# The row maximum of a causal attention taken over the newest 512 keys of a chunk, on a signal of its own

## The chip, the cores and the metric

The kernel runs on one core of a Trainium2 chip. The metric is the device time in microseconds (us) of one execution, the median of several.

## The reference

One transformer block with adaptive layer norm on 4096 rows of 256 channels. The attention has 16 heads of 16 channels. What matters here:

```python
h = layernorm(x) * (1 + ca) + sa
q, k, v = split(h @ W_attn)                      # 16 heads of 16 channels, T = 4096
att = softmax(where(causal, q @ k.T / 4, -inf))
att = att * decay_weight_matrix(T)               # 0 from a distance of 512 on
y = (att @ v) @ W_proj
x = x + ga * y                                   # then a second layer norm and a linear layer
```

The softmax sums over all earlier keys, but the decay matrix is 0 beyond a distance of 511, so values are needed for the newest 5 blocks of 128 keys alone.

## The kernel before

Queries are handled in 32 tiles of 128 rows. `attention_fast` works on pairs of tiles: pair p joins a FAR tile (16 + p, which sees 17 + p blocks of 128 keys) with a NEAR tile (15 - p, which sees 16 - p blocks). For each pair and each of 16 heads there is one step, 16 x 16 = 256 steps in all, numbered s. In a step the keys of both tiles are cut into five chunks of at most 1024 keys (`split`, `order`): the newest chunk of the FAR tile first (FAR, 0), an older one of it (FAR, 1), the newest of the NEAR tile (NEAR, 0), and two more older ones. The newest chunk has at least 5 blocks where there are that many: 640 columns for the FAR tile of pairs 0 to 4 and 8 to 12, 768 for pairs 5 and 13, 896 for 6 and 14, 1024 for 7 and 15.

All engines run a list written out by hand, in step order:

- TensorE (PE), `fill` (L839): one chunk of scores into one of three slots of PSUM (`s_ps`, `SLOTS` = 3, each 1024 fp32 columns, two banks of 512), in matmuls of at most 512 columns. Chunk n waits (`exp_done`) until ScalarE is done with chunk n - 3. The newest chunk ends with a 128-column matmul (L856) that adds the causal mask to its last block. Then `s_full` is raised. Between the fills stand the transposes of the exponentials (`turn` L871 for three blocks, `turn_tail` L887 for the other two), in every second step the products with the values for a group of four heads (`values`, L902, in two parts), and the jobs that finish the pair before (projection, second norm, linear layer; L913, L923, L931, L944).
- VectorE (DVE), `maximum` (L1076): waits for `s_full`, then a minimum over the last 640 columns of the newest chunk (the scores carry a negative scale), L1082, and raises `max_done`. `decay` (L1091) and `decay_tail` (L1101) multiply the transposed exponentials by the decay while they move them out of PSUM. The order in a step is: maximum FAR of step s; decay and decay_tail of NEAR of step s - 1; maximum NEAR of s; small jobs; decay FAR of s; a copy of a finished group (L1107) or another job; decay_tail FAR of s.
- ScalarE (ACT), `exponential` (L1011, L1029): one activation for each chunk, with the maximum as bias and a sum over the row. That of a newest chunk waits for `max_done` and for the transposes of the step before, and writes `probs` in SBUF; the others wait for `s_full` and write back into the slot.

The maximum only keeps the exponentials within the range of fp32. The sums over a row are compared with SUM_LIMIT = 1e37 at the end; if one is above, `attention_full` and `rest_full` compute everything again (`again > 0`).

```python
dve.wait_ge(s_full, n + 1)
nc.vector.tensor_reduce(out=negmax[:, p % 2, side, h:h + 1],
                        in_=s_ps[:, n % SLOTS, max(0, cols - P * WIN):cols],
                        axis=AX_X, op=ALU.min).then_inc(max_done, 1)
```

Of the kernel before, what the change touches and what calls it, by code (L numbers as in the profile page):

```python
# [5 lines left out]
def bass_adaln_block_kernel(nc, x, w_attn, w_proj, ffn_wT, ffn_b, lora_downT, lora_upT, down_aux, up_auxT,  # L6
# [18 lines left out]
    P = 128  # L25
# [3 lines left out]
    NH, HD = 16, 16  # L29
# [12 lines left out]
    BANK = 512  # L42
    CW = 2 * BANK
    RING = 3
    WIN = 5
# [149 lines left out]
    with ctx:  # L195
# [3 lines left out]
        def sem(name):  # L199
            return ctx.enter_context(nc.semaphore(name))  # L200
# [426 lines left out]
        def attention_fast():  # L627
# [22 lines left out]
            def split(i):  # L650

                nb = i + 1
                n = -(-nb // CB)
                first = nb if n == 1 else max(WIN, nb - CB * (n - 1))
                cuts = [(nb - first, nb)]
                left = nb - first
                while left > 0:
                    cuts.append((max(0, left - CB), left))
                    left = cuts[-1][0]
                return cuts  # L660

            def order(p):

                if len(split(tile_of(p, NEAR))) == 1:
                    return [(FAR, 0), (FAR, 1), (NEAR, 0), (FAR, 2), (FAR, 3)]
                return [(FAR, 0), (FAR, 1), (NEAR, 0), (NEAR, 1), (FAR, 2)]
# [60 lines left out]
            vals_loaded = [sem(f"fast_vals_loaded{b}") for b in range(2)]  # L727
            decay_loaded = sem("fast_decay_loaded")
            s_full = sem("fast_s_full")
            max_done = sem("fast_max_done")  # L730
            exp_done = sem("fast_exp_done")
            turn_full = sem("fast_turn_full")
# [24 lines left out]
            with s2:  # L757
# [80 lines left out]
                def _(pe):  # L838
                    def fill(s, pos):  # L839

                        p, h = step_of(s)
                        side, c = order(p)[pos]
                        i = tile_of(p, side)
                        n = PER * s + pos
                        if n >= SLOTS:
                            pe.wait_ge(exp_done, n - SLOTS + 1)
                        b0, b1 = split(i)[c]
                        cols = P * (b1 - b0)
                        q = q_stack[:, s // QH % 2, side, s % QH, :]
                        for o in range(0, cols, BANK):  # L850
                            w = min(BANK, cols - o)
                            diag = c == 0 and o + w == cols
                            last = nc.tensor.matmul(s_ps[:, n % SLOTS, o:o + w], q, k_stack[:, h, P * b0 + o:P * b0 + o + w],  # L853
                                                    start=True, stop=not diag)
                            if diag:
                                last = nc.tensor.matmul(s_ps[:, n % SLOTS, o + w - P:o + w], ident_b[:], causal[:],  # L856
                                                        start=False, stop=True)
                        last.then_inc(s_full, 1)

                    def turn(side, s):  # L860
# [148 lines left out]
                @block.scalar  # L1009
                def _(act):  # L1010
                    def exponential(s, pos):  # L1011
                        p, h = step_of(s)
                        side, c = order(p)[pos]
                        n = PER * s + pos
                        b0, b1 = split(tile_of(p, side))[c]
                        cols = P * (b1 - b0)
                        src = dst = s_ps[:, n % SLOTS, 0:cols]
                        if c == 0:
                            act.wait_ge(max_done, 2 * s + side + 1)
                            if s > 0:  # L1020

                                if has_tail(side, s - 1):
                                    act.wait_ge(tail_full, tail_no["unit", side, s - 1] + 1)
                                else:
                                    act.wait_ge(turn_full, turn_no["unit", side, s - 1] + 1)
                            dst = probs[:, side, 0:cols]
                        else:
                            act.wait_ge(s_full, n + 1)
                        nc.scalar.activation(dst, src, ACT.Exp, bias=negmax[:, p % 2, side, h:h + 1], scale=-1.0,  # L1029
                                             accum_out=sums[:, p % 2, side, h, c:c + 1]).then_inc(exp_done, 1)  # L1030

                    for s in range(NSTEP):
                        for pos in range(PER):
                            exponential(s, pos)
# [35 lines left out]
                def _(dve):  # L1070
# [5 lines left out]
                    def maximum(side, s):  # L1076
                        p, h = step_of(s)
                        n = PER * s + order(p).index((side, 0))
                        dve.wait_ge(s_full, n + 1)
                        b0, b1 = split(tile_of(p, side))[0]  # L1080
                        cols = P * (b1 - b0)
                        nc.vector.tensor_reduce(out=negmax[:, p % 2, side, h:h + 1],  # L1082
                                                in_=s_ps[:, n % SLOTS, max(0, cols - P * WIN):cols],
                                                axis=AX_X, op=ALU.min).then_inc(max_done, 1)

                    def decay(side, s):
# [809 lines left out]
```

## Time and profile before

| what | value |
| --- | --- |
| median of 3 runs | 1506.9 us (1505.77 to 1508.43) |
| the profiled execution | 1504.86 us |
| its span, first to last instruction | 1502.3 us |
| ScalarE busy | 1298.8 us (86%) |
| TensorE matmuls busy | 1263.3 us (84%) |
| VectorE busy | 1000.9 us (67%) |
| first and last exponential start | 164.66 us, 1466.46 us |

The first 165 us are the layer norm, the projections and the splitting of q and k into bf16 parts; the last 35 us finish the last pair. Between them run the 256 steps of attention. A line number such as L1082 is a line of the kernel before. "PE" rows are matmuls, "PEld" rows are weight loads. A row of the timeline gives start, duration, engine, line and operation, and in brackets how long the engine had been idle before it and what ended that.

### The profile page before, as it was taken

Reading aid. Unit: us, or ns where it says so; the run is one execution under the profiler, and the core shown is the slowest. Engines: PE = TensorE matmul, PEld = TensorE weight load, DVE = VectorE, ACT = ScalarE, POOL = GpSimd, SP = SyncE. Lnnn points to the kernel's source line nnn. Section 1 sums busy time; section 2 is a strip of 40 time slices with the busy share of each in tenths; the row PEclk is TensorE's granted clock in tenths of the full one; section 3 lists DMA queues with packets and bytes.
Section 4 is the critical chain, followed back from the end, with each engine's and each line's share of the span. In section 5 each row is a group of like instructions: output and inputs, shape, how many; then the busy total and the mean of one; then the engine's idle time right before and its main releaser. Section 6 shows DMA issues by size and latency. Waiting matters only on the chain.

```text
span 1502.3 us, 28806 instructions
## 1 busy us (share of the span) xinstructions
PE 1263.3 (84%) x11067; PEld 745.0 (50%) x11067; DVE 1000.9 (67%) x2058; ACT 1298.8 (86%) x2628; POOL 204.2 (14%) x429
## 2 busy tenths in 40 slices
PE   7994588989888898888888998988898888887774
PEld 5552345555555555555555555555555444444432
DVE  4843477777777777777777777777776766665452
ACT  2552699999999999999999999999999999999880
POOL 0331000110202020202011020202020201111022
PEclk9996799999999999999999999999999999999996
DMA  4797300000000000000000000000000000000000
GB/s 154 240 302 263 106 12 12 19 26 19 15 19 14 23 19 26 19 25 19 26 19 23 17 14 22 16 26 19 26 16 25 15 26 15 26 15 19 8 4 13
DMA packets 94448, 64.63 MB, mean 43 GB/s; under 512 B 59595, under 2 KB 89570, under 8 KB 94306
## 3 DMA queue, kind: packets, MB, share of 16 engines
q1 hardware_dynamic: 94306, 62.75, 14.1%
q8 instruction: 87, 1.43, 0.4%
q14 instruction: 55, 0.45, 0.1%
HBM read 41.74 MB, written 20.97 MB: 42 GB/s over the span
## 4 chain that ended last, share of the span: by engine, by line
PE 39%; DVE 27%; ACT 13%; issue 9%; POOL 1%; SPq 0%; DMA 0%; ACTq 0%; DVEq 0%
PE fast_s_ps L853 13%; DVE fast_negmax L1082 12%; PE fast_t_ps L902 10%; ACT fast_s_ps L1029 8%; DVE fast_probsT L1101 7%; PE fast_t_ps L871 5%; PE fast_t_ps L887 5%; ACT fast_probs L1029 5%; PE fast_t_ps L931 4%; DVE fast_probsT L1091 4%; DVE fast_y_sb L1120 1%; DVE fast_xb L1134 1%; DVE fast_xb L1157 1%; PE fast_t_ps L913 1%; DVE fast_tT L1127 1%
## 5 line engine op out<-in xcount | busy, mean ns | idle before, releaser
L1029 ACT ACTIVATE fast_s_ps<-fast_s_ps,fast_negmax 128x1024 f32<-128x1024 f32 (+4 forms) x768 | 786.6, 1026 | 12.4 <-PE fast_s_ps L853 11.7
L853 PE MATMUL fast_s_ps<-k_stack,fast_q_stack 96*128 96x512 bf16 (+3 forms) x2448 | 643.2, 354 | 118.1 <-ACT fast_probs L1029 83.5
L1029 ACT ACTIVATE fast_probs<-fast_s_ps,fast_negmax 128x640 f32<-128x640 f32 (+7 forms) x512 | 431.7, 843 | 62.1 <-DVE fast_negmax L1082 57.8
L1082 DVE TENSOR_REDUCE fast_negmax<-fast_s_ps 128x1 f32<-128x640 f32 (+4 forms) x512 | 397.9, 777 | 35.9 <-PE fast_s_ps L856 20.2
L1091 DVE TENSOR_TENSOR fast_probsT<-fast_t_ps,fast_dec_c 128x384 f32<-128x384 f32 (+2 forms) x512 | 276.6, 540 | 202.8 <-PE fast_t_ps L871 202.7
L853 PEld LDWEIGHTS fast_s_ps<-k_stack,fast_q_stack 96*128 96x128 bf16 x2448 | 202.4, 98 | 321.4 <-ACT fast_probs L1029 137.2
L871 PE MATMUL fast_t_ps<-ident,fast_probs 128*128 128x128 f32 x1488 | 252.0, 276 | 29.4 <-DVE fast_y_sb L1120 20.8
L1101 DVE TENSOR_TENSOR fast_probsT<-fast_t_ps,fast_dec_c 128x256 f32<-128x256 f32 x464 | 192.4, 415 | 114.7 <-PE fast_t_ps L887 114.7
L871 PEld LDWEIGHTS fast_t_ps<-ident,fast_probs 128*128 128x128 f32 x1488 | 171.8, 142 | 84.1 <-DVE fast_y_sb L1120 28.1
L887 PE MATMUL fast_t_ps<-ident,fast_probs 128*128 128x128 f32 x912 | 195.9, 295 | 19.9 <-DVE fast_tT L1127 6.4
L902 PE MATMUL fast_t_ps<-fast_probsT,fast_vals 128*16 128x128 f32 x4800 | 179.8, 275 | 23.4 <-DVE fast_probsT L1101 21.9
L1029 ACT ACTIVATION_READ_ACCUMULATOR fast_s_ps<-fast_s_ps,fast_negmax 128x1 f32 x768 | 163.6, 213 | 0.0
L1048 POOL TENSOR_SCALAR fast_var_e<-fast_mv 128x1 f32<-128x1 f32 x32 | 7.3, 228 | 1129.5 <-DVE fast_mv L1142 1129.4
L887 PEld LDWEIGHTS fast_t_ps<-ident,fast_probs 128*128 128x128 f32 x912 | 97.2, 141 | 118.7 <-DVE fast_yT_sb L1107 47.9
L902 PEld LDWEIGHTS fast_t_ps<-fast_probsT,fast_vals 128*16 128x16 f32 x4800 | 109.1, 96 | 71.3 <-DVE fast_probsT L1101 45.8
L856 PE MATMUL fast_s_ps<-causal,ident_b 128*128 128x128 bf16 x512 | 113.3, 221 | 0.0
L1029 ACT ACTIVATION_READ_ACCUMULATOR fast_probs<-fast_s_ps,fast_negmax 128x1 f32 x512 | 104.2, 203 | 0.0
L856 PEld LDWEIGHTS fast_s_ps<-causal,ident_b 128*128 128x128 bf16 x512 | 49.8, 97 | 54.9 <-issue 1.4
L392 ACT CAST part<-kq 128x2048 bf16<-128x2048 f32 x8 | 15.2, 1898 | 39.7 <-issue 20.2
L404 POOL TENSOR_TENSOR part<-kq,part 128x2048 bf16<-128x2048 f32 (+1 forms) x8 | 32.0, 4000 | 103.2 <-ACT part L392 103.2
L1054 POOL TENSOR_SCALAR fast_rstd<-fast_root_t,fast_three_halves,fast_rstd 128x1 f32<-128x1 f32 x128 | 44.0, 344 | 12.9
L1053 POOL TENSOR_SCALAR fast_root_t<-fast_rstd,fast_var_h 128x1 f32<-128x1 f32 x128 | 44.0, 344 | 12.9
(110 smaller groups left out, 723.7 us busy)
## 6 DMA issues: line engine op xcount, KB each, us to landing
parts_d<-part SPq DMA_DIRECT2D x24, 512.0 KB, 4.3
k_stack<-parts_d SPq DMA_DIRECT2D x96, 128.0 KB, 3.0
fast_q_stack<-parts_d SPq DMA_DIRECT2D x384, 32.0 KB, 2.1
fast_vals<-v_d SPq DMA_DIRECT2D x36, 128.0 KB, 2.5
xs<-x_dram SPq DMA_DIRECT2D x8, 512.0 KB, 6.6
v_d<-w SPq DMA_DIRECT2D x8, 512.0 KB, 5.7
fast_xb<-x_dram SPq DMA_DIRECT2D x32, 128.0 KB, 2.1
out_dram<-fast_xb SPq DMA_DIRECT2D x32, 128.0 KB, 2.0
```

The lines of the kernel that those rows point to most:

```text
L853: last = nc.tensor.matmul(s_ps[:, n % SLOTS, o:o + w], q, k_stack[:, h, P * b0 + o:P * b0 + o + w], start=True, stop=not diag)
L856: last = nc.tensor.matmul(s_ps[:, n % SLOTS, o + w - P:o + w], ident_b[:], causal[:], start=False, stop=True)
L871: last = nc.tensor.transpose(t_ps[:, P * b:P * (b + 1)], probs[:, side, lo:lo + P], ident[:])
L887: last = nc.tensor.transpose(tail_ps[:, P * (b - HEAD):P * (b - HEAD + 1)], probs[:, side, lo:lo + P], ident[:])
L902: last = nc.tensor.matmul(g_ps[TC * j:TC * j + HD, :], vals[:, side, (i + 1 - nb + b) % VT, HD * (h + j):HD * (h + j + 1)], probsT[:, turn ...
L931: last = nc.tensor.matmul(tail_ps[:, 0:C], tT[:, side, cc, :], weights[:, cc, :], start=(cc == 0), stop=(cc == CH - 1))
L1029: nc.scalar.activation(dst, src, ACT.Exp, bias=negmax[:, p % 2, side, h:h + 1], scale=-1.0, accum_out=sums[:, p % 2, side, h, c:c + 1]).th ...
L1053: chained(nc.gpsimd.tensor_scalar(w, y, y, half, ALU.mult, ALU.mult))
L1054: chained(nc.gpsimd.tensor_scalar(y, w, three_halves[:, 0:1], y, ALU.add, ALU.mult))
L1082: nc.vector.tensor_reduce(out=negmax[:, p % 2, side, h:h + 1], in_=s_ps[:, n % SLOTS, max(0, cols - P * WIN):cols], axis=AX_X, op=ALU.min) ...
L1091: nc.vector.tensor_tensor(probsT[:, turned(side, s), 0:n, :], t_ps[:, 0:P * n].rearrange("p (b q) -> p b q", q=P), dec_c[:, WIN - nb:WIN - ...
L1101: nc.vector.tensor_tensor(probsT[:, turned(side, s), HEAD:nb, :], tail_ps[:, 0:P * (nb - HEAD)].rearrange("p (b q) -> p b q", q=P), dec_c[ ...
```

## The change

In a newest chunk the columns now lie at the end of the slot (CW - cols to CW) and no longer at its start. The matmul over its newest 512 columns comes first, then the causal mask; if the chunk has more than 4 blocks, a new semaphore `new_full` is raised there, and a matmul over the older columns follows, after which `s_full` is raised. The maximum waits for `new_full` instead of `s_full` and reads the newest 512 columns instead of 640. The exponential of such a chunk waits for `s_full` too. Tiles whose newest chunk has at most 4 blocks keep their wait. Older chunks are filled as before.

```diff
--- before.py
+++ after.py
@@ -659,6 +659,19 @@
                     left = cuts[-1][0]
                 return cuts
 
+            MAXW = BANK // P
+
+            def has_older_part(s, side):
+
+                b0, b1 = split(tile_of(s // NH, side))[0]
+                return b1 - b0 > MAXW
+
+            new_no = {}
+            for s in range(NSTEP):
+                for side in (FAR, NEAR):
+                    if has_older_part(s, side):
+                        new_no[side, s] = len(new_no)
+
             def order(p):
 
                 if len(split(tile_of(p, NEAR))) == 1:
@@ -727,6 +740,7 @@
             vals_loaded = [sem(f"fast_vals_loaded{b}") for b in range(2)]
             decay_loaded = sem("fast_decay_loaded")
             s_full = sem("fast_s_full")
+            new_full = sem("fast_new_full")
             max_done = sem("fast_max_done")
             exp_done = sem("fast_exp_done")
             turn_full = sem("fast_turn_full")
@@ -847,14 +861,21 @@
                         b0, b1 = split(i)[c]
                         cols = P * (b1 - b0)
                         q = q_stack[:, s // QH % 2, side, s % QH, :]
-                        for o in range(0, cols, BANK):
-                            w = min(BANK, cols - o)
-                            diag = c == 0 and o + w == cols
-                            last = nc.tensor.matmul(s_ps[:, n % SLOTS, o:o + w], q, k_stack[:, h, P * b0 + o:P * b0 + o + w],
-                                                    start=True, stop=not diag)
-                            if diag:
-                                last = nc.tensor.matmul(s_ps[:, n % SLOTS, o + w - P:o + w], ident_b[:], causal[:],
-                                                        start=False, stop=True)
+
+                        def scores(at, k0, w, stop=True):
+                            return nc.tensor.matmul(s_ps[:, n % SLOTS, at:at + w], q, k_stack[:, h, k0:k0 + w], start=True, stop=stop)
+
+                        if c > 0:
+                            for o in range(0, cols, BANK):
+                                last = scores(o, P * b0 + o, min(BANK, cols - o))
+                            last.then_inc(s_full, 1)
+                            return
+                        w = min(BANK, cols)
+                        scores(CW - w, P * b1 - w, w, stop=False)
+                        last = nc.tensor.matmul(s_ps[:, n % SLOTS, CW - P:CW], ident_b[:], causal[:], start=False, stop=True)
+                        if has_older_part(s, side):
+                            last.then_inc(new_full, 1)
+                            last = scores(CW - cols, P * b0, cols - BANK)
                         last.then_inc(s_full, 1)
 
                     def turn(side, s):
@@ -1014,9 +1035,11 @@
                         n = PER * s + pos
                         b0, b1 = split(tile_of(p, side))[c]
                         cols = P * (b1 - b0)
-                        src = dst = s_ps[:, n % SLOTS, 0:cols]
+                        src = dst = s_ps[:, n % SLOTS, CW - cols:CW] if c == 0 else s_ps[:, n % SLOTS, 0:cols]
                         if c == 0:
                             act.wait_ge(max_done, 2 * s + side + 1)
+                            if has_older_part(s, side):
+                                act.wait_ge(s_full, n + 1)
                             if s > 0:
 
                                 if has_tail(side, s - 1):
@@ -1076,11 +1099,13 @@
                     def maximum(side, s):
                         p, h = step_of(s)
                         n = PER * s + order(p).index((side, 0))
-                        dve.wait_ge(s_full, n + 1)
+                        if has_older_part(s, side):
+                            dve.wait_ge(new_full, new_no[side, s] + 1)
+                        else:
+                            dve.wait_ge(s_full, n + 1)
                         b0, b1 = split(tile_of(p, side))[0]
-                        cols = P * (b1 - b0)
                         nc.vector.tensor_reduce(out=negmax[:, p % 2, side, h:h + 1],
-                                                in_=s_ps[:, n % SLOTS, max(0, cols - P * WIN):cols],
+                                                in_=s_ps[:, n % SLOTS, CW - P * min(MAXW, b1 - b0):CW],
                                                 axis=AX_X, op=ALU.min).then_inc(max_done, 1)
 
                     def decay(side, s):
```

How the instructions move, first on TensorE. This is the start of a step: the fill of (FAR, 0), the transposes of NEAR of the step before, and the first matmul of the next fill (names ending in k_stack, q_stack are the score matmuls; causal, ident_b is the mask). Before:

```order
L853 MATMUL fast_s_ps<-k_stack,fast_q_stack 128x512 [waits fast_exp_done]
L853 MATMUL fast_s_ps<-k_stack,fast_q_stack 128x128
L856 MATMUL fast_s_ps<-causal,ident_b 128x128
L871 MATMUL fast_t_ps<-ident,fast_probs 128x128 [waits fast_turn_free]
L871 MATMUL fast_t_ps<-ident,fast_probs 128x128 x2
L887 MATMUL fast_t_ps<-ident,fast_probs 128x128 [waits fast_tail_free]
L887 MATMUL fast_t_ps<-ident,fast_probs 128x128
L853 MATMUL fast_s_ps<-k_stack,fast_q_stack 128x512 [waits fast_exp_done]
```

After:

```order
L866 MATMUL fast_s_ps<-k_stack,fast_q_stack 128x512 [waits fast_exp_done]
L875 MATMUL fast_s_ps<-causal,ident_b 128x128
L866 MATMUL fast_s_ps<-k_stack,fast_q_stack 128x128
L892 MATMUL fast_t_ps<-ident,fast_probs 128x128 [waits fast_turn_free]
L892 MATMUL fast_t_ps<-ident,fast_probs 128x128 x2
L908 MATMUL fast_t_ps<-ident,fast_probs 128x128 [waits fast_tail_free]
L908 MATMUL fast_t_ps<-ident,fast_probs 128x128
L866 MATMUL fast_s_ps<-k_stack,fast_q_stack 128x512 [waits fast_exp_done]
```

The mask has moved ahead of the 128 older columns; the number and the sizes of the matmuls, and all that follows, stay as they were.

On VectorE, the end of one step and the start of the next, where the maximum stands behind the group's copy and `decay_tail` FAR. Before:

```order
L1107 COPY fast_yT_sb<-fast_t_ps 128x128 [waits fast_tail_full]
L1101 TENSOR_TENSOR fast_probsT<-fast_t_ps,fast_dec_c 128x256 [waits fast_tail_full]
L1082 TENSOR_REDUCE fast_negmax<-fast_s_ps 128x1 [waits fast_s_full]
L1091 TENSOR_TENSOR fast_probsT<-fast_t_ps,fast_dec_c 128x384 [waits fast_turn_full]
L1101 TENSOR_TENSOR fast_probsT<-fast_t_ps,fast_dec_c 128x256 [waits fast_tail_full]
L1082 TENSOR_REDUCE fast_negmax<-fast_s_ps 128x1 [waits fast_s_full]
```

After:

```order
L1132 COPY fast_yT_sb<-fast_t_ps 128x128 [waits fast_tail_full]
L1126 TENSOR_TENSOR fast_probsT<-fast_t_ps,fast_dec_c 128x256 [waits fast_tail_full]
L1107 TENSOR_REDUCE fast_negmax<-fast_s_ps 128x1 [waits fast_new_full]
L1116 TENSOR_TENSOR fast_probsT<-fast_t_ps,fast_dec_c 128x384 [waits fast_turn_full]
L1126 TENSOR_TENSOR fast_probsT<-fast_t_ps,fast_dec_c 128x256 [waits fast_tail_full]
L1107 TENSOR_REDUCE fast_negmax<-fast_s_ps 128x1 [waits fast_new_full]
```

The place of the maximum in the list is the same; its wait is now for the first 512 columns.

On ScalarE, five exponentials in a row, two of them of newest chunks (they write fast_probs). Before:

```order
L1029 ACTIVATE fast_s_ps,fast_sums<-fast_s_ps,fast_negmax 128x1024 [waits fast_s_full]
L1029 ACTIVATE fast_probs,fast_sums<-fast_s_ps,fast_negmax 128x640 [waits fast_tail_full,fast_max_done]
L1029 ACTIVATE fast_s_ps,fast_sums<-fast_s_ps,fast_negmax 128x768 [waits fast_s_full]
L1029 ACTIVATE fast_s_ps,fast_sums<-fast_s_ps,fast_negmax 128x1024 [waits fast_s_full]
L1029 ACTIVATE fast_probs,fast_sums<-fast_s_ps,fast_negmax 128x768 [waits fast_tail_full,fast_max_done]
```

After:

```order
L1052 ACTIVATE fast_s_ps,fast_sums<-fast_s_ps,fast_negmax 128x1024 [waits fast_s_full]
L1052 ACTIVATE fast_probs,fast_sums<-fast_s_ps,fast_negmax 128x640 [waits fast_tail_full,fast_s_full,fast_max_done]
L1052 ACTIVATE fast_s_ps,fast_sums<-fast_s_ps,fast_negmax 128x768 [waits fast_s_full]
L1052 ACTIVATE fast_s_ps,fast_sums<-fast_s_ps,fast_negmax 128x1024 [waits fast_s_full]
L1052 ACTIVATE fast_probs,fast_sums<-fast_s_ps,fast_negmax 128x768 [waits fast_tail_full,fast_s_full,fast_max_done]
```

The two exponentials of newest chunks have one wait more.

## Rows read from the trace of the kernel before

**Rows 1.** The page, part 4: the chain that ended last, by line.

```profile
PE fast_s_ps L853 13%; DVE fast_negmax L1082 12%; PE fast_t_ps L902 10%; ACT fast_s_ps L1029 8%; DVE fast_probsT L1101 7%; PE fast_t_ps L871 5%; PE fast_t_ps L887 5%; ACT fast_probs L1029 5%; PE fast_t_ps L931 4%; DVE fast_probsT L1091 4%; DVE fast_y_sb L1120 1%; DVE fast_xb L1134 1%; DVE fast_xb L1157 1%; PE fast_t_ps L913 1%; DVE fast_tT L1127 1%
```

**Rows 2.** 243 to 1141 us: length, busy (x count) of PE, PEld, DVE, ACT, POOL, clock.

```profile
243.00:1141.20 898.20, 794.81 (x7713) 481.06 (x7712) 661.92 (x1332) 852.76 (x1761) 118.16 (x286) 1.00 0.08 20
```

**Rows 3.** Waits, whole span: who waited for whom, us in total, times, longest.

```profile
ACT fast_probs L1029 <- DVE fast_negmax L1082: 57.8, 141, 10.6
...
DVE fast_negmax L1082 <- PE fast_s_ps L856: 20.2, 52, 1.4
```

**Rows 4.** Timeline of ScalarE, 521 to 525 us (pair 4).

```profile
521.22 1.10 ACT L1029 ACTIVATE fast_s_ps<-fast_s_ps,fast_negmax 128x1024 f32<-128x1024 f32 x1
522.22 0.22 ACT L1029 ACTIVATION_READ_ACCUMULATOR fast_s_ps<-fast_s_ps,fast_negmax 128x1 f32 x1
522.72 0.80 ACT L1029 ACTIVATE fast_probs<-fast_s_ps,fast_negmax 128x640 f32<-128x640 f32 x1 [0.28 <-DVE fast_negmax L1082]
...
523.50 1.08 ACT L1029 ACTIVATE fast_s_ps<-fast_s_ps,fast_negmax 128x1024 f32<-128x1024 f32 x1
...
524.59 0.79 ACT L1029 ACTIVATE fast_probs<-fast_s_ps,fast_negmax 128x640 f32<-128x640 f32 x1
```

**Rows 5.** Timeline of ScalarE: (FAR, 0) and the row before, first and last of 255 steps.

```profile
168.71 0.67 ACT L1029 ACTIVATE fast_s_ps<-fast_s_ps,fast_negmax 128x512 f32<-128x512 f32 x1
...
169.66 0.79 ACT L1029 ACTIVATE fast_probs<-fast_s_ps,fast_negmax 128x640 f32<-128x640 f32 x1 [0.16 <-DVE fast_negmax L1082]
...
1461.59 1.10 ACT L1029 ACTIVATE fast_s_ps<-fast_s_ps,fast_negmax 128x1024 f32<-128x1024 f32 x1
...
1462.84 1.11 ACT L1029 ACTIVATE fast_probs<-fast_s_ps,fast_negmax 128x1024 f32<-128x1024 f32 x1
```

**Rows 6.** Chain in order of time, 516 to 529 us (pair 4): start, us, what.

```profile
516.83 0.73 DVE fast_negmax L1082
517.56 0.46 DVE fast_probsT L1091
518.03 0.34 DVE fast_probsT L1101
...
518.41 0.85 PE fast_t_ps L902 x24
...
521.52 0.42 DVE fast_probsT L1101
521.95 0.74 DVE fast_negmax L1082
...
522.72 0.22 ACT fast_probs L1029
...
523.66 0.55 PE fast_s_ps L853 x2
...
526.82 0.73 DVE fast_negmax L1082
...
528.40 0.85 PE fast_t_ps L902 x24
```

**Rows 7.** Lines by form, DVE: count, busy, mean ns, idle before.

```profile
L1082 DVE TENSOR_REDUCE fast_negmax<-fast_s_ps 128x1 f32<-128x640 f32 x448 | 366.7, 819 | 30.4 <-PE fast_s_ps L856 16.1 <-PE fast_s_ps L853 10.6
...
L1082 DVE TENSOR_REDUCE fast_negmax<-fast_s_ps 128x1 f32<-128x512 f32 x16 | 11.0, 686 | 0.2 <-PE fast_s_ps L856 0.2
```

**Rows 8.** Timeline of DVE, pair 4: decay_tail FAR, then the maximum FAR.

```profile
521.52 0.42 DVE L1101 TENSOR_TENSOR fast_probsT<-fast_t_ps,fast_dec_c 128x256 f32<-128x256 f32 x1 [0.53 <-PE fast_t_ps L887]
521.87 0.82 DVE L1082 TENSOR_REDUCE fast_negmax<-fast_s_ps 128x1 f32<-128x640 f32 x1
```

**Rows 9.** Timeline of PE, pair 4: the mask ahead of that maximum.

```profile
521.60 0.22 PE L856 MATMUL fast_s_ps<-causal,ident_b 128*128 128x128 bf16 x1
```

**Rows 10.** Timeline of DVE, pair 7 (1024 columns): decay_tail FAR, then the maximum.

```profile
787.89 0.42 DVE L1101 TENSOR_TENSOR fast_probsT<-fast_t_ps,fast_dec_c 128x256 f32<-128x256 f32 x1 [0.53 <-PE fast_t_ps L887]
788.38 0.82 DVE L1082 TENSOR_REDUCE fast_negmax<-fast_s_ps 128x1 f32<-128x640 f32 x1
```

## The prediction

> **What bounds the kernel now.** I read the chain of the page first, by line: the maximum (L1082) has 12% of it, though VectorE is busy for 67% of the span only [rows 1]. So a reduction on a half idle engine is part of what sets the time. Then the stretch of pairs 1 to 11: in 898.2 us ScalarE is busy for 852.8, 95%, TensorE's matmuls for 794.8, VectorE for 661.9, at a granted clock of 1.00, the 2.4 GHz level [rows 2]. ScalarE is nearly the bound, and what the change can give at most is what ScalarE still waits. The list of waits says for whom: exponentials of newest chunks for the maximum, 57.8 us, of which 10.6 is one wait at the very start; 47.2 us over 140 waits remain [rows 3].
>
> The timeline shows that the loss is larger than "idle". The activation at 521.22 ends at 522.32 and the next one starts at 522.72, a hole of 0.40, of which 0.28 is booked as idle, since the read of the accumulator (0.22 from 522.22) stands in it. Without a wait the next activation starts as the last one ends: 522.72 + 0.80 = 523.52 against a start at 523.50 [rows 4]. I took this hole ahead of (FAR, 0) for steps 1 to 255, from start times like those of the first and the last [rows 5], 0.28 and 0.15; the sum over the 255 is 76 us. The holes before (NEAR, 0), read in the same way, sum to under 2 us. **76 us is the ceiling.**
>
> The chain in order of time then says what makes (FAR, 0) late. In one step it runs: maximum FAR (516.83), decay and decay_tail of NEAR (517.56, 518.03), values (518.41), then TensorE's list without a gap up to decay_tail FAR (521.52), and again maximum FAR (521.95). In the next it runs from that maximum to the exponential (522.72), the fill that needs its slot (523.66), a projection, decay_tail, and the maximum at 526.82, after which decay, decay_tail and values (528.40) follow again [rows 6]. The loop of two steps holds **two maxima of the FAR tile**, and no maximum of the NEAR tile. ScalarE is in it for one exponential out of ten. So what comes off a FAR maximum comes off the period, until the holes on ScalarE are used up.
>
> **The change, part by part.** *The shorter reduction.* 640 columns take 819 ns (448 of them), 512 columns 686 ns (16 of them) [rows 7], so each of the 448 loses 0.133 us, 60 us of VectorE in all. The 192 on the NEAR side lie beside exponentials that don't wait, and count as 0; if the cover went, they would be worth 192 x 0.133 = 26 us more at most. On the FAR side it is one for each step: 256 x 0.133 = **34.0 us**.
>
> *The early signal.* In pair 4 decay_tail FAR starts at 521.52 and takes 0.42, and the maximum starts at 521.87, that is 0.07 before the end of that row [rows 8]; the mask ends at 521.82 [rows 9]. VectorE and TensorE arrive together, and VectorE is as early as it can be: an earlier signal gives nothing there. That is so in the ten pairs with 640 FAR columns, 160 steps. With 1024 columns the maximum starts 0.07 after the end of decay_tail (788.38 against 787.89 + 0.42 = 788.31) [rows 10], 0.14 later than in pair 4; with 896 and 768 columns I read about 0.10 and 0.04. There are two pairs of each, 32 steps: 32 x (0.14 + 0.10 + 0.04) = **9.0 us**. The end below is 0. The end above is that the 128-column matmul counts also in the 160 steps. The trace doesn't show it alone; two score matmuls start and end within 0.5 us, and I put it at 0.05: 8 us more.
>
> *Where ScalarE has no hole left.* Taking steps two by two, since the loop is of two, the gain is the smaller of both holes and twice the step's saving. Done for all 255 this costs 2.6 us against the two terms, mostly in pairs 13 and 14, where every second hole is near 0: **-2.6 us**.
>
> *The third wait.* The exponential of a newest chunk waits for `s_full` too, which has long come when the reduction ends: the rest of the fill is 128 to 512 columns, the reduction 0.69 us. What stays is the look at one semaphore more. No row shows a third wait; one with two starts 0.01 after the end of the one before (523.50 + 1.08, 524.59), one with a single wait 0.02 before it (522.72 + 0.80, 523.50) [rows 4]. I take 0.02 on the 139 exponentials that wait, **-2.8 us**, between 0 and, if it hit all 448, -9 us.
>
> *The rest.* The matmuls are as many and as wide, each with its own weight load as before; the order mask, older part instead of older part, mask costs nothing, and no DMA moves. Behind the mask on TensorE's queue nothing is later, since the whole fill takes as long. On VectorE the maximum has the same place; what is queued behind it (decay of NEAR, waited for by the values) comes 0.133 earlier, which is the gain itself.
>
> Sum: 34.0 + 9.0 - 2.6 - 2.8 = 37.6 us, 2.5%. The profiled execution took 1504.9 us (span 1502.3 and 2.6 around it): 1467.3. The median is 2.0 above it, so the forecast is **1469 us**. With the ends of the terms the gain lies between 34.0 - 2.6 - 9 = 22 and 34.0 + 9.0 + 8 = 51, 1456 to 1485. A difference under 0.2%, 3 us, could not be told from none.
>
> **A rule that speaks against it.** The rows name ScalarE as the busiest engine, and the change takes nothing off its work. The Trainium skill (Perfetto Trace Analysis, "Identifying the Most-Contended Engine") says to optimise the most-contended engine first, taken as the one with the highest occupancy. By that the sum would be 0 and the time 1506.9. The hole at 522.72, with the maximum named as what ends it [rows 4], is what speaks against the rule here.
>
> **The rivals.** *Only the visible waits shrink.* The period doesn't shrink with both maxima, since something else arrives just as late (the fill that waits for an exponential, or TensorE's list, 88% busy [rows 2]). Then each of the 140 waits [rows 3] loses 0.133 once: 19 us, 1488. For it: in most second steps the hole is 0.2 or less. Against: the chain has both maxima with nothing between them and the values.
>
> *Hidden.* ScalarE's neighbours fill the time again, 0 gained, 1507, as the rule on the busiest engine would have it.
>
> *All holes close.* The time gained moves TensorE's waits apart so that more than the maximum comes early: up to 76 us, 1431; a part of it, 60 us, is 1447. For it: none of the chain's pieces, only that waits of the kind "both arrive together" can give way in both directions.
>
> *Slower: the reduction is disturbed.* TensorE now writes the lower bank of the slot while VectorE reads the upper one. If that made the reduction of 512 columns take more than the 0.82 of now, the loop would be longer: at 0.92 by 256 x 0.10 = 26 us, 1533; the point is 0.82. Against: TensorE's matmuls are busy for 88% of the time [rows 2], so they write beside nearly all of today's reductions, which average 819 ns [rows 7] and take 0.82 in each row shown [rows 8, 10].
>
> *Slower: everything twice.* With a maximum over fewer keys a row's sum could pass 1e37, whose logarithm is 85.2, and the attention of at least 1300 us would run again, over 2800 us. I worked out the sums from the inputs and the reference's formulas: the largest logarithm is 61.9 with 5 blocks and 68.7 with 4. So it isn't taken.
>
> **How the numbers follow.** The loop as worked out: 0.67. Only the visible waits: 0.17. More than 51 us: 0.08. Hidden: 0.04. Disturbed: 0.03; twice: 0.01. Faster is 0.67 + 0.17 + 0.08 = 0.92, same 0.04, slower 0.04. The range takes the first case with its ends, 1456 to 1485, and the second, up to 1489; below I go to 1450, which takes in a small part of the third.
>
> **What would show it.** Reductions of 512 columns at 0.69 us. ScalarE's waits for the maximum down from 57.8 to about 30 us, the start of 10.6 included. The 16 steps of pair 4 shorter by about 2 us, those of pair 7 by over 4. The maximum in pair 7 starting 0.07 before the end of decay_tail, as in pair 4. No wait of the exponential for `s_full`. I am wrong if the chain no longer holds the maximum twice in two steps and the time is above 1489, if the reduction of 512 columns takes much over 0.69, or if the wide pairs gain no more than the narrow ones.

## The result and the profile after

The changed kernel takes 1463.0 us (median of 4 runs, 1459.68 to 1464.15), the kernel before on the same chip 1506.3. The ratio is 0.9715, with a 95% interval of 0.9696 to 0.9734: 43 us less, where 37.6 were forecast.

In what follows, "the changed kernel" is this one. Line numbers have moved with the change: the score matmuls are L866 (were L853), the mask L875 (L856), the transposes L892 and L908 (L871, L887), the values L923 (L902), the exponential L1052 (L1029), the maximum L1107 (L1082), decay and decay_tail L1116 and L1126 (L1091, L1101).

The chain by line, of the page of the kernel after, answers to [rows 1]:

```profile
PE fast_s_ps L866 14%; ACT fast_s_ps L1052 10%; ACT fast_probs L1052 9%; PE fast_t_ps L923 8%; DVE fast_negmax L1107 6%; PE fast_t_ps L892 6%; PE fast_t_ps L908 6%; DVE fast_probsT L1126 5%; PE fast_t_ps L952 4%; DVE fast_probsT L1116 3%; DVE fast_xb L1182 1%; DVE fast_y_sb L1145 1%; DVE fast_xb L1159 1%; DVE fast_tT L1152 1%; DVE fast_tT L1176 1%
```

The maximum has 6% of the chain, where it had 12%. The stretch of pairs 1 to 11, from the first exponential of pair 1 to that of pair 12, in the columns of [rows 2] (length, busy time and count of PE, PEld, DVE, ACT, POOL, clock, DMA share, GB/s):

```profile
242.96:1111.93 868.97, 794.78 (x7713) 483.06 (x7712) 612.41 (x1332) 847.29 (x1762) 117.44 (x286) 1.00 0.08 21
```

It is 869.0 us long instead of 898.2. TensorE and VectorE run as many instructions as before (7713 matmuls, 1332 rows), but VectorE is busy for 49.5 us less (612.4 against 661.9). ScalarE is busy for 97.5% of the stretch instead of 95. The waits that answer to [rows 3], and the reduction by form that answers to [rows 7]:

```profile
DVE fast_negmax L1107 <- PE fast_s_ps L875: 26.1, 63, 0.9
...
ACT fast_probs L1052 <- DVE fast_negmax L1107: 16.3, 57, 0.9
```

```profile
L1107 DVE TENSOR_REDUCE fast_negmax<-fast_s_ps 128x1 f32<-128x512 f32 x464 | 317.0, 683 | 25.3 <-PE fast_s_ps L875 13.4 <-DMA fast_dec_c<-decay_cols_dram 10.5
```

ScalarE waits 16.3 us for the maximum. Before, it was 47.2 without the one wait of 10.6 at the start, which the trace of the changed kernel books on another line. The reduction takes 683 ns instead of 819.

The chain in order of time again, at the same steps of pair 4 (as [rows 6]: start, us, what):

```profile
506.25 0.55 PE fast_s_ps L866 x2
...
507.17 0.56 DVE fast_probsT L1116
507.73 0.61 DVE fast_tT L1152
...
508.38 0.44 PE fast_t_ps L908 x2
...
509.19 0.96 ACT fast_s_ps L1052 x2
510.15 0.78 ACT fast_probs L1052 x2
510.93 1.09 ACT fast_s_ps L1052 x2
512.02 0.78 ACT fast_probs L1052 x2
512.80 1.38 ACT fast_s_ps L1052 x3
...
514.90 0.67 ACT fast_probs L1052
...
518.58 0.42 DVE fast_probsT L1126
519.00 0.60 DVE fast_negmax L1107
519.60 0.47 DVE fast_probsT L1116
520.07 0.34 DVE fast_probsT L1126
...
520.45 0.85 PE fast_t_ps L923 x24
```

Here the chain stays on ScalarE from 509.19 on, for one whole step of exponentials (0.45 us of it is booked as issue, in the rows left out). Before, in [rows 6], ScalarE was in it once in two steps. Where holes are left, the old loop is still seen: maximum (519.00), decay, decay_tail, values.

### The profile page after: what moved, and what is told of

It is laid out like the page before. It is cut to its first block, busy times and chain, and to the rows that moved or that the text cites. A ratio compares the mean times of both kernels' runs of the same rounds, so it can differ in the third digit from the quotient of the medians.

```text
span 1460.6 us, 28808 instructions
## 1 busy us (share of the span) xinstructions
PE 1260.3 (86%) x11067; PEld 747.5 (51%) x11067; DVE 936.9 (64%) x2058; ACT 1289.9 (88%) x2628; POOL 203.1 (14%) x429
## 4 chain that ended last, share of the span: by engine, by line
PE 39%; DVE 19%; ACT 19%; issue 5%; POOL 1%; ACTq 0%; DVEq 0%
PE fast_s_ps L866 14%; ACT fast_s_ps L1052 10%; ACT fast_probs L1052 9%; PE fast_t_ps L923 8%; DVE fast_negmax L1107 6%; PE fast_t_ps L892 6%; PE fast_t_ps L908 6%; DVE fast_probsT L1126 5%; PE fast_t_ps L952 4%; DVE fast_probsT L1116 3%; DVE fast_xb L1182 1%; DVE fast_y_sb L1145 1%; DVE fast_xb L1159 1%; DVE fast_tT L1152 1%; DVE fast_tT L1176 1%
## 5 line engine op out<-in xcount | busy, mean ns | idle before, releaser
L1052 ACT ACTIVATE fast_s_ps<-fast_s_ps,fast_negmax 128x1024 f32<-128x1024 f32 (+4 forms) x768 | 789.5, 1032 | 8.6 <-PE fast_s_ps L866 8.1
L866 PE MATMUL fast_s_ps<-k_stack,fast_q_stack 96*128 96x512 bf16 (+3 forms) x2448 | 667.9, 353 | 94.4 <-ACT fast_probs L1052 60.2
L1052 ACT ACTIVATE fast_probs<-fast_s_ps,fast_negmax 128x640 f32<-128x640 f32 (+7 forms) x512 | 433.8, 847 | 21.4 <-DVE fast_negmax L1107 16.3
L1116 DVE TENSOR_TENSOR fast_probsT<-fast_t_ps,fast_dec_c 128x384 f32<-128x384 f32 (+2 forms) x512 | 276.7, 540 | 221.2 <-PE fast_t_ps L892 221.1
L866 PEld LDWEIGHTS fast_s_ps<-k_stack,fast_q_stack 96*128 96x128 bf16 x2448 | 208.9, 98 | 337.2 <-ACT fast_probs L1052 112.8
L1107 DVE TENSOR_REDUCE fast_negmax<-fast_s_ps 128x1 f32<-128x512 f32 (+3 forms) x512 | 337.4, 659 | 38.3 <-PE fast_s_ps L875 26.1
L892 PE MATMUL fast_t_ps<-ident,fast_probs 128*128 128x128 f32 x1488 | 251.0, 275 | 28.0 <-DVE fast_y_sb L1145 19.4
L1126 DVE TENSOR_TENSOR fast_probsT<-fast_t_ps,fast_dec_c 128x256 f32<-128x256 f32 x464 | 192.5, 415 | 114.7 <-PE fast_t_ps L908 114.7
L892 PEld LDWEIGHTS fast_t_ps<-ident,fast_probs 128*128 128x128 f32 x1488 | 177.1, 141 | 78.0 <-DVE fast_y_sb L1145 26.5
L908 PE MATMUL fast_t_ps<-ident,fast_probs 128*128 128x128 f32 x912 | 195.5, 295 | 20.1 <-DVE fast_tT L1152 6.4
L923 PE MATMUL fast_t_ps<-fast_probsT,fast_vals 128*16 128x128 f32 x4800 | 179.7, 275 | 9.0 <-DVE fast_probsT L1126 4.5
L1052 ACT ACTIVATION_READ_ACCUMULATOR fast_s_ps<-fast_s_ps,fast_negmax 128x1 f32 x768 | 168.4, 219 | 0.0
L908 PEld LDWEIGHTS fast_t_ps<-ident,fast_probs 128*128 128x128 f32 x912 | 96.8, 141 | 118.5 <-DVE fast_yT_sb L1132 48.0
L923 PEld LDWEIGHTS fast_t_ps<-fast_probsT,fast_vals 128*16 128x16 f32 x4800 | 109.0, 96 | 56.3 <-DVE fast_probsT L1126 28.4
L875 PE MATMUL fast_s_ps<-causal,ident_b 128*128 128x128 bf16 x512 | 112.9, 220 | 0.0
L1052 ACT ACTIVATION_READ_ACCUMULATOR fast_probs<-fast_s_ps,fast_negmax 128x1 f32 x512 | 107.5, 210 | 0.0
L875 PEld LDWEIGHTS fast_s_ps<-causal,ident_b 128*128 128x128 bf16 x512 | 50.2, 98 | 16.0 <-issue 0.5
```

Source lines behind the costliest of these rows:

```text
L866: return nc.tensor.matmul(s_ps[:, n % SLOTS, at:at + w], q, k_stack[:, h, k0:k0 + w], start=True, stop=stop)
L875: last = nc.tensor.matmul(s_ps[:, n % SLOTS, CW - P:CW], ident_b[:], causal[:], start=False, stop=True)
L892: last = nc.tensor.transpose(t_ps[:, P * b:P * (b + 1)], probs[:, side, lo:lo + P], ident[:])
L908: last = nc.tensor.transpose(tail_ps[:, P * (b - HEAD):P * (b - HEAD + 1)], probs[:, side, lo:lo + P], ident[:])
L923: last = nc.tensor.matmul(g_ps[TC * j:TC * j + HD, :], vals[:, side, (i + 1 - nb + b) % VT, HD * (h + j):HD * (h + j + 1)], probsT[:, turn ...
L1116: nc.vector.tensor_tensor(probsT[:, turned(side, s), 0:n, :], t_ps[:, 0:P * n].rearrange("p (b q) -> p b q", q=P), dec_c[:, WIN - nb:WIN - ...
```

## The experiments

All of them are compared with the kernel before on the same chip; each ratio has its 95% interval. For the stretch of the 256 steps I also give how much shorter a pair of tiles is than before, from the start of its first exponential to the start of the next pair's (for pair 15, to the end of the last exponential). These lengths are read from the profiled execution of each kernel. A "narrow" pair has 640 columns in the newest FAR chunk, a "wide" one 768 to 1024.

### The shorter reduction without the signal of its own

```diff
-                        if has_older_part(s, side):
-                            dve.wait_ge(new_full, new_no[side, s] + 1)
-                        else:
-                            dve.wait_ge(s_full, n + 1)
+                        dve.wait_ge(s_full, n + 1)
```

> The changed kernel without its own signal: the maximum over 512 columns waits for the whole chunk again. Loop theory: nothing is lost in the ten pairs with 640 FAR columns, since decay_tail FAR on VectorE ends together with the fill; 32 x (0.14 + 0.10 + 0.04) = 9 us are lost in the six wide ones, so 1463 + 9 = 1472 us, and in pair 7 the maximum starts 0.07 after the end of decay_tail, in pair 4 0.08 before it. Rival A, the signal counts in every step (0.05 for the 128-column matmul): 1480. Rival B, the signal is worth nothing: 1463.

1472.6 us, ratio 0.9795 (0.9769 to 0.9821). (`new_full` isn't raised in it either.) The signal is worth 12 us by the ratios (0.9795 - 0.9715 of 1504) and 9.6 by the medians. The two ratios stand against different executions of the kernel before, and their intervals together leave about 5 us open to each side. Maximum and decay_tail in pair 7, in this kernel and then in the changed one (in the first, L1122 is decay_tail and L1103 the maximum; in the changed one, L1126 and L1107):

```profile
766.01 0.43 DVE L1122 TENSOR_TENSOR fast_probsT<-fast_t_ps,fast_dec_c 128x256 f32<-128x256 f32 x1 [0.53 <-PE fast_t_ps L907]
766.50 0.69 DVE L1103 TENSOR_REDUCE fast_negmax<-fast_s_ps 128x1 f32<-128x512 f32 x1
```

```profile
739.69 0.42 DVE L1126 TENSOR_TENSOR fast_probsT<-fast_t_ps,fast_dec_c 128x256 f32<-128x256 f32 x1 [0.53 <-PE fast_t_ps L908]
740.03 0.68 DVE L1107 TENSOR_REDUCE fast_negmax<-fast_s_ps 128x1 f32<-128x512 f32 x1
```

With the wait for the whole chunk the maximum starts 0.06 after the end of decay_tail (766.01 + 0.43 = 766.44), as in [rows 10]; with the signal of its own it starts 0.08 before it (739.69 + 0.42 = 740.11), as it does in pair 4. In pairs 5, 6 and 7 the changed kernel is 3.15, 3.98 and 4.57 us shorter than before, this one 2.18, 2.20 and 2.19. The difference, 1.0, 1.8 and 2.4, stands against a forecast of 0.6, 1.6 and 2.2 (16 steps each by 0.04, 0.10 and 0.14). In the narrow pairs 1 to 4 and 8 to 12 the signal gives 0.1 to 0.2 us for 16 steps: 0.01 us a step, close to nothing. The rival that priced it at 0.05 in every step wanted 0.8.

Of the wide pairs at the end only pair 13 (0.5 us) can be used. In pairs 14 and 15 the difference is 2.2 and 3.0, but there the granted clock of this execution fell to 0.50 for some 3 us, once in each, and that of the changed kernel did not:

```profile
1338.60:1341.80 3.20, 3.20 (x10) 1.76 (x9) 1.15 (x3) 1.29 (x3) 0.00 (x0) 0.50 0.01 3
1420.60:1423.60 3.00, 3.00 (x9) 1.89 (x9) 0.98 (x2) 0.89 (x2) 0.00 (x0) 0.50 0.00 0
```

### The place and the order alone

```diff
-                                                in_=s_ps[:, n % SLOTS, CW - P * min(MAXW, b1 - b0):CW],
+                                                in_=s_ps[:, n % SLOTS, CW - P * min(WIN, b1 - b0):CW],
```

with the wait of the experiment above: the maximum is again over 640 columns and after the whole chunk.

> New place in the slot, newest 512 columns and mask first, but the maximum over 640 columns and after the whole chunk, as before. Loop theory: placing and order cost and give nothing, 1506 us as before, within 3 us; at most 9 us slower if the third wait of the exponential is paid by all 448. Rival: the order of the matmuls itself brought part of the 43 us (mask earlier, other banks), then under 1500.

1503.1 us, ratio 1.000 (0.9981 to 1.0019). Mask first, newest part first and the other place in the slot cost nothing and give nothing that can be told, and the third wait of the exponential is in this kernel too. The waits of ScalarE for the maximum are those of before:

```profile
ACT fast_probs L1051 <- DVE fast_negmax L1103: 48.2, 140, 1.0
```

Pairs 1 to 14 differ from before by 0.1 us at most, and are 0.6 us longer in all. Pair 0 is 0.4 us longer. Pair 15 is 3.5 us shorter, of which below.

### The FAR maxima alone

```diff
-                        if has_older_part(s, side):
+                        if side == FAR and has_older_part(s, side):
                             dve.wait_ge(new_full, new_no[side, s] + 1)
...
-                                                in_=s_ps[:, n % SLOTS, CW - P * min(MAXW, b1 - b0):CW],
+                                                in_=s_ps[:, n % SLOTS, CW - P * min(MAXW if side == FAR else WIN, b1 - b0):CW],
```

> The changed kernel, but only the FAR maxima take 512 columns and the new signal; the 192 NEAR maxima with 5 or more blocks read 640 columns after the whole chunk. Loop theory: the loop holds no NEAR maximum, so all of the gain stays, 1463 us within 3. Rival, each of the 448 shortened maxima counts alike: 192 of 448 of 43 us are lost, 1481.

1464.3 us, ratio 0.9742 (0.9715 to 0.9769), an interval that overlaps that of the changed kernel. Its reductions by form:

```profile
L1108 DVE TENSOR_REDUCE fast_negmax<-fast_s_ps 128x1 f32<-128x512 f32 x272 | 185.4, 682 | 20.2 <-DMA fast_dec_c<-decay_cols_dram 10.6 <-PE fast_s_ps L875 8.5
L1108 DVE TENSOR_REDUCE fast_negmax<-fast_s_ps 128x1 f32<-128x640 f32 x192 | 157.7, 821 | 12.0 <-PE fast_s_ps L866 9.3
```

192 reductions have their 0.82 us back, 26 us of work on VectorE, and the stretch of the steps is 1.5 us longer than in the changed kernel (1261.6 against 1260.1).

### The NEAR maxima alone

The same edit with NEAR in place of FAR.

> The opposite: only the NEAR maxima take 512 columns and the new signal. Loop theory: 1506 us as before, within 3. Rival, each of the 448 counts alike: 1506 - 18 = 1488.

1503.0 us, ratio 0.9995 (0.9982 to 1.0008). Its reductions of 640 and 512 columns:

```profile
L1108 DVE TENSOR_REDUCE fast_negmax<-fast_s_ps 128x1 f32<-128x640 f32 x256 | 210.3, 821 | 25.5 <-PE fast_s_ps L866 22.2
L1108 DVE TENSOR_REDUCE fast_negmax<-fast_s_ps 128x1 f32<-128x512 f32 x208 | 141.6, 681 | 1.9 <-PE fast_s_ps L875 0.5
```

The 26 us taken off VectorE here are worth nothing, or 0.1 us a pair. With the experiment above: the gain is the FAR maxima's, all of it but 0.1 us a pair.

How much shorter than before the pairs are, in us. A star marks a pair in which the granted clock of that execution fell to 0.50 for some us. In the kernel before it did so in pair 15:

| kernel | 1 to 4, each | 5 | 6 | 7 | 8 to 11, each | 12 | 13 | 14 | 15 |
| --- | --- | --- | --- | --- | --- | --- | --- | --- | --- |
| changed | 2.2 to 2.3 | 3.15 | 3.98 | 4.57 | 2.0 to 2.2 | 1.9 | 1.7 | 2.2 | 7.1 |
| without the signal | 2.0 to 2.1 | 2.18 | 2.20 | 2.19 | 1.9 to 2.1 | 1.8 | 1.2 | 0.0* | 4.1* |
| FAR alone | 2.0 to 2.2 | 3.04 | 3.84 | 4.41 | 1.8 to 2.1 | 2.0 | 1.7 | 2.2 | 7.1 |
| NEAR alone | 0.1 | 0.11 | 0.09 | 0.08 | 0.1 | 0.0 | -1.4* | 0.0 | 3.5 |

### Another 128 columns less

```diff
-                                                in_=s_ps[:, n % SLOTS, CW - P * min(MAXW, b1 - b0):CW],
+                                                in_=s_ps[:, n % SLOTS, CW - P * min(3, b1 - b0):CW],
```

> The changed kernel with the maximum over the newest 384 columns instead of 512 (the sums of a row stay below the limit: the largest logarithm, worked out from the inputs, is 68.7 for 3 blocks as for 4, against 85.2). Loop theory: another 0.13 us off each FAR maximum; by the holes left on ScalarE in the changed kernel, two steps taken together, 25 us of the 33 can be had: 1438 us, about 0.96 of before. Rival, the rest of the holes has another cause: 1463, no change. Rival, only each hole by itself shrinks: 19 us, 1444.

1440.0 us, ratio 0.957 (0.9551 to 0.959): 23 us less than the changed kernel by the medians, 22 by the ratios, where 25 were expected. The reductions, ScalarE's waits, and pairs 1 to 11:

```profile
L1107 DVE TENSOR_REDUCE fast_negmax<-fast_s_ps 128x1 f32<-128x384 f32 x480 | 265.4, 553 | 38.3 <-PE fast_s_ps L875 22.6 <-DMA fast_dec_c<-decay_cols_dram 10.6
```

```profile
ACT fast_probs L1052 <- DVE fast_negmax L1107: 5.4, 15, 0.7
```

```profile
240.30:1090.70 850.40, 793.16 (x7713) 482.34 (x7712) 576.86 (x1332) 840.43 (x1762) 117.47 (x286) 1.00 0.08 21
```

The stretch is 850.4 us long (869.0 in the changed kernel), and ScalarE is busy for 98.8% of it. The sum of the holes ahead of (FAR, 0), counted as in the forecast, went from 76 us before to 37 in the changed kernel and 13 here: by 24 in this last step, and the steps as a whole became 22.7 us shorter (1260.1 to 1237.4).

### The price of a met wait

```diff
                                 act.wait_ge(s_full, n + 1)
+                            act.wait_ge(k_last, 32 * len(PAIRS))
+                            act.wait_ge(decay_loaded, 16)
```

> The changed kernel with two waits more on each exponential of a newest chunk, on semaphores that were met long before. The forecast priced one more wait at 0.02 us on the exponentials that wait for the maximum. If that price is right, two more cost 0.04 x 512 at most, 20 us, and about 4 us if only those that wait pay: 1467. If a met wait costs nothing: 1463 within 3.

Both semaphores were met long before. 1462.0 us, ratio 0.9716 (0.9697 to 0.9735), that of the changed kernel. The maximum and the exponential behind it, with five waits (L1109, L1054), then with three:

```profile
523.11 0.68 DVE L1109 TENSOR_REDUCE fast_negmax<-fast_s_ps 128x1 f32<-128x512 f32 x1
...
523.83 0.79 ACT L1054 ACTIVATE fast_probs<-fast_s_ps,fast_negmax 128x640 f32<-128x640 f32 x1
```

```profile
475.12 0.68 DVE L1107 TENSOR_REDUCE fast_negmax<-fast_s_ps 128x1 f32<-128x512 f32 x1
...
475.83 0.79 ACT L1052 ACTIVATE fast_probs<-fast_s_ps,fast_negmax 128x640 f32<-128x640 f32 x1 [0.20 <-DVE fast_negmax L1107]
```

The start comes 0.04 and 0.03 after the end of the reduction (523.79, 475.80), as before the change (522.69 to 522.72, in [rows 4] and [rows 8]). Pairs 1 to 14, with 448 of these exponentials, take 1103.5 us in both kernels, the same to 0.1 us. A wait that is met costs nothing that can be told here.

### The last holes: a job moved by a step

7.7 of the 13 us left in the 384-column kernel stand ahead of step 14 of a pair. In step 13 two jobs come together: the linear layer of the FAR tile, and the transposes of the second norm of the NEAR tile. The second is moved, in the 384-column kernel.

```diff
-            HEAD_JOBS = {1: ("back", FAR), 3: ("back", NEAR), 13: ("n_turn", NEAR)}
+            HEAD_JOBS = {1: ("back", FAR), 3: ("back", NEAR), 14: ("n_turn", NEAR)}
```

> The kernel with the maximum over 384 columns (1440 us), and the transposes of the second norm of the NEAR tile moved from step 13 of a pair, which also has the linear layer of the FAR tile, to step 14. In the 384-column kernel 7.7 of the 13 us of holes left ahead of (FAR, 0) stand ahead of step 14. If they come from the two jobs in step 13, they go: 1440 - 6 = 1434 us. Rival: step 14 has a group of values, and the job only makes the next step late; the holes move to step 15, 1440.

1438.9 us, ratio 0.9575 (0.9562 to 0.9588): no gain over 0.957. The rival was right in the main. The holes ahead of step 14 sum to 0.5 us now, those ahead of step 15 to 5.7 instead of 1.7, and the last fill of step 14 comes late. Pairs 1 to 14 are 1.1 us shorter together than in the 384-column kernel, not 6; pair 15 is 2.3 us longer, with the granted clock down for some us in this execution. ScalarE in pair 2, from (FAR, 0) of step 14 to that of step 15:

```profile
385.99 0.81 ACT L1052 ACTIVATE fast_probs<-fast_s_ps,fast_negmax 128x640 f32<-128x640 f32 x1
...
390.45 0.88 ACT L1052 ACTIVATE fast_s_ps<-fast_s_ps,fast_negmax 128x768 f32<-128x768 f32 x1 [0.48 <-PE fast_s_ps L866]
...
391.80 0.80 ACT L1052 ACTIVATE fast_probs<-fast_s_ps,fast_negmax 128x640 f32<-128x640 f32 x1 [0.35 <-DVE fast_negmax L1107]
```

> The same, with that job moved to step 12 instead. The normalised rows come from GpSimd, which starts after the statistics in step 11 and takes about 6 us for a side, more than a step. If they are ready in step 12, 1434 us as with step 14; if not, TensorE waits for them up to some us in each of 15 pairs, with everything queued behind it, and it is slower than 1440: 2 us for each pair would give 1470.

With 12 instead of 14: 1449.0 us, ratio 0.9646 (0.9633 to 0.9659), 9 us slower than the 384-column kernel. Pairs 1 to 13 are longer by 0.6 to 0.8 us each, not by the 2 us of the estimate. TensorE waits 16 times for GpSimd's normalised rows in this kernel, and twice in the 384-column one (first row this kernel, then that one):

```profile
PE fast_t_ps L965 <- POOL fast_y_sb L1085: 17.6, 16, 5.9
```

```profile
PE fast_t_ps L965 <- POOL fast_y_sb L1085: 10.3, 2, 5.9
```

## Why the prediction was right, and where it was off

The forecast was 1469 us and a gain of 37.6; the kernel took 1463.0 and gained 43.

**The bound and the loop** were as read. The loop of two steps has two FAR maxima and no NEAR one: FAR alone gives the whole gain, NEAR alone 0.1 us a pair, and a second cut by the same 128 columns gives what the holes left allow.

**The shorter reduction**, 34.0 us forecast, is 0.133 x 16 = 2.1 us a pair. The changed kernel is shorter by 2.2, 2.2, 2.2 and 2.3 us in pairs 1 to 4, and by 2.0, 2.2, 2.2 and 2.2 in pairs 8 to 11. Pair 0 is only 0.6 us shorter; in the other kernels with the shorter FAR maximum over 512 columns it is 0.8 to 1.0. The forecast gave it 2.1 like the rest, and why it gains less is open.

**The early signal**, 9.0 us forecast and nothing in the narrow pairs: shown by the first experiment, best by the pairs: 5.1 us against 4.5 in pairs 5 to 7, and 0.1 to 0.2 a narrow pair. The 9.6 us of the medians lie near the forecast, the 12 of the ratios above it; the intervals do not part them, and two falls of the clock stand in the profiled execution without the signal.

**Where ScalarE has no hole left**, -2.6 us: pairs 12, 13 and 14 are 1.9, 1.7 and 2.2 us shorter. The forecast's sums for them were 1.9, 2.1 and 3.0, so the holes run out there as it said, and cost 1.2 us more in these three pairs than it took off.

**The third wait**, -2.8 us, is the term that was wrong. It was read out of 0.03 us of difference between starts that follow each other. Two waits more changed nothing to 0.1 us over pairs 1 to 14, and the third wait together with the new order (the second experiment) costs 0.6 us there. Without the term the forecast would have been 40.4 us.

**How 40.4 compares with 43.** The 16 pairs together are 42.8 us shorter in the profiled execution. Pair 15 alone is 7.1 us shorter, where 4.3 were worked out. In the kernel before, the granted clock fell there, twice. Its windows, in the columns of [rows 2], and the last pairs of the kernel with place and order alone:

```profile
1301.00:1396.00 95.00, 76.38 (x660) 40.66 (x653) 55.55 (x126) 90.92 (x189) 10.74 (x26) 1.00 0.10 26
1400.00:1404.00 4.00, 3.62 (x13) 2.12 (x14) 1.66 (x4) 1.83 (x4) 0.00 (x0) 0.50 0.00 0
```

```profile
1298.00:1462.00 164.00, 128.24 (x1059) 69.11 (x1058) 91.72 (x210) 155.32 (x321) 21.34 (x52) 1.00 0.06 16
```

Before, it fell from 1.00 to 0.50, the lower of its levels (1.2 GHz), which it had from 1400 to 1404, and again near 1454. Ahead of the first fall TensorE had stood idle for ScalarE twice:

```profile
1396.90 0.23 PE L853 MATMUL fast_s_ps<-k_stack,fast_q_stack 96*128 96x128 bf16 x1 [0.38 <-ACT fast_s_ps L1029]
...
1398.14 0.87 PE L853 MATMUL fast_s_ps<-k_stack,fast_q_stack 96*128 96x512 bf16 x2 [0.94 <-ACT fast_probs L1029]
```

In the kernel of the second experiment, which does the same work, the clock stayed at 1.00, and pair 15 was 3.5 us shorter. It had the same idle times at the same place, so these alone do not explain the fall:

```profile
1398.12 0.23 PE L866 MATMUL fast_s_ps<-k_stack,fast_q_stack 96*128 96x128 bf16 x1 [0.37 <-ACT fast_s_ps L1051]
...
1399.36 0.60 PE L866 MATMUL fast_s_ps<-k_stack,fast_q_stack 96*128 96x512 bf16 x2 [0.95 <-ACT fast_probs L1051]
```

So some 3.5 of the 7.1 us are falls of the clock that one execution had and another not, and not the change; 39.3 of the 42.8 are left, against 40.4. In the changed kernel the clock stood at 1.00 there:

```profile
1266.00:1425.00 159.00, 128.79 (x1062) 69.31 (x1060) 86.00 (x212) 154.45 (x323) 21.34 (x52) 1.00 0.06 17
```

The medians say the same. In 37 executions of the kernel before, those that stand beside the experiments, the time goes with the mean granted clock: 1499.9 us at 0.975, 1507.9 to 1509.2 at 0.966 and 0.967. The 13 of them at 0.972 or 0.973 average 1502.4, and the four of the changed kernel, all at 0.972 or 0.973, 1462.5: 40 us less. That the forecast gain of 37.6 was 6 us low is thus, as far as these runs show, 2.8 of the third wait and some 3 of the clock, which the forecast did not have in it. Whether the changed kernel has fewer such falls because it waits less, no run shows.

**The rivals.** "Only the visible waits shrink" (1488, 19 us off) fell: the holes ahead of (FAR, 0) alone shrank by 39 us. "Hidden" fell: ScalarE's work was not touched, and 2.85% went. The Trainium skill (Perfetto Trace Analysis, "Identifying the Most-Contended Engine") says that the most-contended engine is to be optimised first; this trace does not bear it out as a rule on the work of that engine, since all of the gain came from reductions on VectorE that start or end sooner, and VectorE was busy for 74% of the stretch before. The Trainium skill (Perfetto Trace Analysis, "Optimization Strategy") also says to find the gaps between slices on that engine and what they wait for. That fits here: the gaps were the holes ahead of (FAR, 0), 76 us before and 37 after. "All holes close": 37 of 76 us are left. "The reduction is disturbed": it takes 683 ns, against 686 for 512 columns in [rows 7], so not. But its condition was hardly met. In most steps of the narrow pairs the matmul of the older part ends 0.04 us before the reduction starts, and in pair 7, where it is 512 columns wide, it ends 0.12 after that start (740.15 against 740.03 above):

```profile
739.77 0.38 PE L866 MATMUL fast_s_ps<-k_stack,fast_q_stack 96*128 96x512 bf16 x1
```

Pairs 4 and 7 both have 682 ns on average. What a longer overlap in one slot would cost is not shown.

"Everything twice" happened neither with 4 blocks nor with 3. With 2 blocks the largest logarithm, worked out from the inputs, is 86.6, above 85.2, and that kernel wasn't run.

## What to carry to other kernels

Follow the chain over a whole period, here two steps, and count how often an instruction stands in it: that number times what is taken off it is the gain, until the holes of the busiest engine, counted from end to start and not as "idle", are used up. An earlier signal is worth only the time that the reader's engine would otherwise stand still; look at whether the reader's preceding instruction ends before or after the signal. Before you compare a pair of profiles to a microsecond, look at the granted clock of each stretch. A cut on an engine that is idle for a quarter of the time can be worth all of itself in one place (FAR) and nothing in another (NEAR).

## What was not expected

A wait for a semaphore that is already met showed no cost on an activation, with up to five of them on one. And the recorded duration of an activation grew from kernel to kernel, as the holes went: 128x1024 (into `s_ps`) took 1091 ns on average before, 1097 in the changed kernel, and 1111 in the 384-column one:

```profile
L1052 ACT ACTIVATE fast_s_ps<-fast_s_ps,fast_negmax 128x1024 f32<-128x1024 f32 x576 | 637.9, 1111 | 6.9 <-PE fast_s_ps L866 6.6
```

Yet from the start of one such activation to the next, where no hole follows, it is 1.09 us in all three kernels. Only the overlap with the next one's row grew, from 2 to 8 to 21 ns on average, so durations summed there overstate the work; starts should be compared. Why it grows is open: in the kernel before, the 1024-column activations with a hole ahead were not the shorter ones (1103 ns against 1093 without).
